# Two tiles of stores in flight, the router judged inside attention's loop, later rests of W2, other row sums on TensorE: one change to a macaron layer (mixture of experts, linear attention, mixture of experts)

## The reference, cut to what matters

```python
def ffn(x):                                # x: [1024, 256]
    shared = silu_and_mul(x @ shared_gate_up_w.T) @ shared_down_w.T    # 704 wide
    shared = shared * sigmoid(x @ sgate_w.T)
    w = softmax(x @ gate_w.T)              # 16 experts
    topk_w, topk_ids = top_k(w, 4)
    for e in range(16):                    # w13_e: [352, 256], w2_e: [256, 176]
        coef = sum(where(topk_ids == e, topk_w, 0.0), axis=-1)
        acc = acc + (silu_and_mul(x @ w13_e.T) @ w2_e.T) * coef
    return shared + acc

x = x + 0.5 * ffn(layernorm(x))
x = x + attention(layernorm(x))            # q, k, v of 2 heads x 128, chunked scan,
x = x + 0.5 * ffn(layernorm(x))            # rmsnorm, Wo
```

## Time and profile before

| what | value |
|---|---|
| median of 3 runs | 455.74 us (454.93 to 457.75) |
| the profiled execution | 455.48 us |
| its span, first to last instruction | 453.7 us |
| TensorE busy | 410.8 us, 91% |
| VectorE busy | 300.4 us, 66% |
| ScalarE busy | 202.1 us, 45% |
| GpSimd busy | 188.9 us, 42% |
| mean granted TensorE clock | 0.951 |
| bytes moved by DMA | 68.17 MB, mean 150 GB/s |

### The profile page before, as it was taken

One profiled execution on the slowest core, in us unless ns is written; L12 is line 12 of the kernel. 1 busy time (PEld: TensorE's weight loads), 2 busy tenths in 40 slices (PEclk: granted clock), 3 DMA queues, 4 the chain that ended last, 5 costly groups with the idle time before them and its releaser, 6 DMA issues.

```text
span 453.7 us, 8744 instructions
## 1 busy us (share of the span) xinstructions
PE 410.8 (91%) x2236; PEld 330.4 (73%) x2239; DVE 300.4 (66%) x943; ACT 202.1 (45%) x564; POOL 188.9 (42%) x199
## 2 busy tenths in 40 slices
PE   5998993699999999978969989689989999999995
PEld 3555552599999999553649975355569999999954
DVE  5666986377777776367596545645767777777637
ACT  2224562266666666124755632001126666666610
POOL 0174846044445445330055300767514544544542
PEclk9988997699999999989998976989999999999999
DMA  7999941344444441660000029422244444444167
GB/s 248 332 281 386 344 136 66 105 136 139 136 148 137 138 144 66 245 252 2 0 0 1 1 73 372 170 104 103 79 119 137 136 138 148 132 145 141 68 242 258
DMA packets 41023, 68.17 MB, mean 150 GB/s; under 512 B 5072, under 2 KB 32208, under 8 KB 40976
## 3 DMA queue, kind: packets, MB, share of 16 engines
q1 hardware_dynamic: 33392, 45.84, 32.4%
q0 software_dynamic: 7584, 21.77, 13.6%
HBM read 42.42 MB, written 25.17 MB: 149 GB/s over the span
## 4 chain that ended last, share of the span: by engine, by line
PE 70%; issue 7%; POOL 6%; DVE 6%; DMA 6%; ACT 3%; SPq 1%; DVEq 0%; POOLq 0%
PE ps L486 7%; PE ps L487 7%; PE ps L490 7%; POOL slots L907 6%; PE ps L426 6%; PE ps L449 5%; PE ps L471 5%; PE ps L431 4%; PE ps L519 3%; PE ps L514 2%; PE ps L518 2%; PE ps L516 2%; PE ps L515 2%; PE ps L497 2%; PE ps L498 2%
## 5 line engine op out<-in xcount | busy, mean ns | idle before, releaser
L914 POOL DMA_INDIRECT rows<-ar,idx x94 | 89.8, 955 | 118.0 <-ACT ar L762 117.4
L907 POOL DMA_INDIRECT slots<-XR,pos x64 | 70.1, 1096 | 76.5 <-DVE pos L1084 41.6
L486 PE MATMUL ps<-WH,xt 128*128 x188 | 69.2, 369 | 0.0
L487 PE MATMUL ps<-WL,xt 128*128 x188 | 61.1, 327 | 0.0
L1127 DVE SCALAR_TENSOR_TENSOR ar<-ps,XR,ar 128x112 f32<-128x112 f32 x94 | 31.4, 334 | 37.9 <-ACT ar L756 37.7
L1143 DVE TENSOR_TENSOR xl<-ps,xt 128x256 fp32r<-128x256 f32 x94 | 39.9, 424 | 24.2 <-ACT xt L751 10.6
L449 PE MATMUL ps<-WS,ar 128*128 128x256 f32 (+1 forms) x192 | 48.4, 399 | 8.1 <-DVE ar L996 7.4
L449 PEld LDWEIGHTS ps<-WS,ar 128*128 128x128 f32 (+1 forms) x192 | 37.3, 197 | 24.7 <-issue 12.9
L756 ACT ACTIVATE ar<-ps 128x176 f32<-128x176 f32 x94 | 29.9, 318 | 51.5 <-PE ps L490 51.5
L426 PE MATMUL ps<-XT,WS 128*128 128x512 f32 x96 | 50.8, 656 | 1.0 <-ACT sgt L739 1.0
L745 ACT ACTIVATE ar<-ps 128x512 f32<-128x512 f32 (+1 forms) x24 | 14.3, 596 | 80.3 <-PE ps L426 80.3
(11 more groups left out here) (171 smaller groups left out, 855.3 us busy)
## 6 DMA issues: line engine op xcount, KB each, us to landing
XR<-slots SPq DMA_DIRECT2D x94, 144.0 KB, 2.1
WR<-w SPq DMA_DIRECT2D x8, 1408.0 KB, 17.1
WR<-rows SPq DMA_DIRECT2D x16, 512.0 KB, 7.3
slots<-zeros SPq DMA_DIRECT2D x1, 2304.0 KB, 12.6
MR<-w2r SPq DMA_DIRECT2D x2, 1024.0 KB, 19.3
MR<-w2m SPq DMA_DIRECT2D x1, 1792.0 KB, 14.3
rows<-ar,idx POOLq DMA_INDIRECT x94, 2.4
X<-x SPq DMA_DIRECT2D x4, 256.0 KB, 4.6
```

The lines of the kernel that those rows point to most:

```text
L486: pe.matmul(to, token, WH[:, bass.ds(e, 1), k, :].rearrange("p a n -> p (a n)"), start=k == 0, stop=False)
L487: pe.matmul(to, token, WL[:, bass.ds(e, 1), k, :].rearrange("p a n -> p (a n)"), start=False, stop=False)
L907: pool.indirect_dma_start(out=slots_dram[:, :], out_offset=bass.IndirectOffsetOnAxis(ap=pos[:, t, r:r + 1], axis=0), in_=XR[:, t, :], in_o ...
L914: pool.indirect_dma_start(out=rows_dram[:, :], out_offset=bass.IndirectOffsetOnAxis(ap=idx[:, i:i + 1], axis=0), in_=ys[i % NY], in_offset ...
```

## The change

**Stores two tiles behind.** `BREAKS` goes. The stores of even and odd tiles count on two semaphores, and before tile t GpSimd waits for the stores of tile t - 2 (and earlier ones of that parity). There are six such waits in a pass where there were two.

**Opening of a pass.** In the first pass `places(0, 0)` comes ahead of the scaling of tiles 4 to 7 on VectorE. TensorE does `ranks(f, 0)` between the two products of unit 0 (`between`). The choice for the second half comes behind unit 0 on VectorE, its places and the table of tiles behind unit 1, `tables` behind unit 3.

**Router in the loop.** `judge(1, 0)` moves to turn 9 of attention's loop on VectorE, `router(1, 0)` to turn 10 on ScalarE.

**Late rests of W2.** `W2_LAST` has three pieces. Experts 0 to 3 stay at unit 7; 4 to 9 and 10 to 15 (`main(8)`, `main(9)`) go on ScalarE ahead of the slots, and on VectorE into the first turn of the slots. VectorE's `shared_sums(f, 1, FRONT)` moves from ahead of the slots to behind the first `left`. TensorE's 8 warming products now also run in the first pass.

**Tail.** TensorE sums the rows of tiles 2 and 3 in the first pass, into banks 0 and 1, between the last `unit_in` and the last two `unit_out`; in the second pass still those of tiles 4 and 5 at the end. Attention's weights come in three loads between the rows, TensorE waits for keys, queries and the rest one by one, and no longer for X of tile 5 before the queries. `gather` is the part of `combine` that makes the sum in SBUF, placed by itself. ScalarE's `norm` asks for the rates of tiles 2 and 3 ahead of the copies of tiles 0 and 1.

```diff
-W2_LAST = {7: (0, 4), 8: (4, NE)}
+W2_LAST = {7: (0, 4), 8: (4, 10), 9: (10, NE)}
-BREAKS = (3, 6)
-BY_PE = (4, 5)
+BY_PE = ((2, 3), (4, 5))
...
-                sp.wait_ge(s_disp, 16 * NT * TOPK * (f + 1))
+                for b in range(2):
+                    sp.wait_ge(s_disp[b], 16 * TOPK * HT * (f + 1))
...
                     if f == 0 and t == 3:
-                        sp.dma_start(WA[:, :, :], wkqv).then_inc(s_wa, 16)
+                        sp.dma_start(WA[:, :, 0:D], wkqv[:, :, 0:D]).then_inc(s_wk, 16)
+                    if f == 0 and t == 5:
+                        sp.dma_start(WA[:, :, D:2 * D], wkqv[:, :, D:2 * D]).then_inc(s_wq, 16)
+                    if f == 0 and t == 7:
+                        sp.dma_start(WA[:, :, 2 * D:], wkqv[:, :, 2 * D:]).then_inc(s_wa, 16)
                         sp.dma_start(WO[:, :, :], woT).then_inc(s_wa, 16)
...
             def rows_summed(f):
-                pe.wait_ge(s_uh, UNITS * (f + 1))
-                for n, t in enumerate(BY_PE):
+                for n, t in enumerate(BY_PE[f]):
...
-                unit_in(f, 0)
-                ranks(f, 0)
+                unit_in(f, 0, lambda: ranks(f, 0))
...
+                unit_in(f, 2)
                 ranks(f, 1)
-                unit_in(f, 2)
                 unit_out(f, 1)
+                unit_in(f, 3)
+                unit_out(f, 2)
                 over_partitions(f)
...
-                if f == 1:
-                    keep_warm(8, 6)
+                keep_warm(8, 6)
...
                 for u in range(FRONT + 1, UNITS):
                     unit_in(f, u)
+                    if f == 0 and u == UNITS - 1:
+                        rows_summed(f)
                     unit_out(f, u - 1)
                 unit_out(f, UNITS - 1)
-                rows_summed(f)
+                if f == 1:
+                    rows_summed(f)
...
             def norm(c):
                 rates(c, 0, 2)
-                for q in range(1, 4):
-                    copied(c, 2 * q - 2)
-                    copied(c, 2 * q - 1)
-                    rates(c, 2 * q, 2)
+                rates(c, 2, 2)
+                for t in range(4):
+                    copied(c, t)
+                rates(c, 4, 2)
...
                 for i in range(3, NT + 5):
                     step(i)
-                router(1, 0)
+                    if i == NT + 2:
+                        router(1, 0)
...
                     for t in range(HT * h, HT * (h + 1)):
-                        if t in BREAKS:
-                            pool.wait_ge(s_disp, 16 * TOPK * (NT * f + t))
+                        wait(pool, s_disp[t % 2], 16 * TOPK * (HT * f + t // 2))
...
                 left(0)
+                shared_sums(f, 1, FRONT)
...
+                    if f == 0 and i == 0:
+                        main(8)
                     if i < TL:
                         hidden(i, e[i])
+                    if f == 0 and i == 0:
+                        main(9)
...
             def ffn(f):
+                unit(f, 0)
                 choose(f, 1)
-                unit(f, 0)
+                unit(f, 1)
                 places(f, 1)
                 tiles_of(f)
-                unit(f, 1)
-                tables(f)
...
-                shared_sums(f, 1, FRONT)
                 slots(f)
...
-                judge(1, 0)
+                    if i == NT + 1:
+                        judge(1, 0)
...
+            places(0, 0)
             for t in range(HT, NT):
                 scale(0, t)
-            places(0, 0)
```

More of the change, by code:

```diff
@@ L428, in unit_in @@
                 mm.then_inc(s_ug, 1)
+                if between:
+                    between()
                 if not last:
@@ L999, in unit, with main @@
                 ins.then_inc(s_uh, 1)
+            def main(u):
+                dve.wait_ge(s_mh, list(W2_LAST).index(u) + 1)
+                for e in range(*W2_LAST[u], 2):
+                    two = slice(e, e + 2)
+                    ins = dve.tensor_tensor(ML[:, two, :], MR[0:FM, two, :], MH[:, two, :].bitcast(F32), ALU.subtract)
+                ins.then_inc(s_ml, 1)
             def part(f, u):
@@ L1007, in part @@
                     ins.then_inc(s_rl, 1)
[L1008 to L1013 removed]
+                if f == 0 and u == 7:
+                    main(u)
                 for e in range(*PARTED.get(u, (0, 0))):
@@ L1223, in ffn @@
                     judge(f, 1)
+                unit(f, 0)
                 choose(f, 1)
-                unit(f, 0)
+                unit(f, 1)
                 places(f, 1)
                 tiles_of(f)
-                unit(f, 1)
-                tables(f)
-                for u in range(2, NJ + 1):
+                unit(f, 2)
+                part(f, 2)
+                for u in range(3, NJ + 1):
                     unit(f, u)
+                    if u == 3:
+                        tables(f)
                     part(f, u)
```

80 lines of the change are left out of this document (48 added, 32 removed).

## The result

| | us | ratio to before |
|---|---|---|
| forecast | 443.2 (438.2 to 449.2) | 0.973 |
| before, beside the changed kernel | 455.34 | 1 |
| changed, first measurement | 483.53 median, 477.63 to 490.43 in 4 runs | 1.051 [1.043, 1.060] |

Medians are of all runs; ratios, and the intervals behind them, compare only the runs that the chip didn't slow down. The same kernel was measured four more times, on chips 9, 2, 10 and 5: 0.981, 0.964, 0.983 and 1.077. So there are two things to explain: what the change is worth where the forecast's picture holds, and the 35 to 45 us that the first and the last of the five measurements add.

The account below looks back on a forecast made before the run. TensorE bounds the slots; the first dispatch, second dispatch and first tail decide the rest. 455.48 - 8.1 (first dispatch) + 2.8 (first slots) - 2.8 (first tail) - 4.2 (second dispatch) = 443.2 us, range 438.2 to 449.2.

Parts of the forecast that it names:

- TensorE's own front: Before the first slot: TensorE's earlier work, with warming products, would end at 73.7, ahead of the slot's start at 75.4.
- E: Rival: stores land in 9.0 us in both dispatches, GpSimd waits before every tile; 457.2 us, chance 3%.
- First dispatch, 8.1 us forecast: First pass's stores: earlier start 1.3 plus drains 9.0 less new waits 2.2; first slot at about 75.4.
- Start 1.3: First dispatch: places come about 1.3 us earlier, no longer behind four scalings and unit 0's second product.
- Drains 9.0: First dispatch: the two drain waits go, 4.32 + 4.69 = 9.0 us.
- New waits 2.2: First dispatch: six waits for stores two tiles back cost 2.2 us in all, bounds 0 and 8.1.
- rival C: VectorE holds GpSimd more than before: two more long stores beside weight splitting cost 3.9 us; 447.1 us, chance 9%.
- First slots, 2.8 given back: First slots: 5.35 us of moved VectorE work, about 2.5 fitting its room, loses 2.8 us.
- First tail, 2.8: First pass's tail: VectorE's 3.9 us wait for ScalarE's rates goes, less 1.1 for a collision; gains 2.8 us.
- the one collision of 1.1: First tail: VectorE held once beside GpSimd's adds of tiles 6, 7, costing 1.1 us, bounds 0 and 2.2.
- Second dispatch, 4.2: Second pass's stores: start 2.0 sooner, drains 2.9 gone, about 0.7 given back in the slots; net 4.2 us.
- The rest at nothing: Second tail, extra DMA issues and tables behind unit 3 were put at no cost or gain.

Follow-up runs that it names:

- e12: Kernel before, unchanged, run again on chip 2 for its profile: 449.96 us, 1.002 of the kernel before.
- e11: Kernel before with only the waits two tiles behind in place of the drains, chip 2: 439.39 us, 0.976 of the kernel before.
- e14: Changed kernel, unchanged, on chip 5: 487.37 us, 1.077 of the kernel before.
- e5: Changed kernel, unchanged, on chip 9: 440.43 us, 0.981 of the kernel before.
- e6: Changed kernel with late rests of W2 and shared sums put back ahead of the slots, chip 9: 436.57 us, 0.970 of the kernel before.
- e10: Same kernel as e6, measured again on chip 2: 434.87 us, 0.967 of the kernel before.
- e16: As e15, with both tails put back too, chip 5: 482.41 us, 1.069 of the kernel before.
- e15: Same kernel as e6, measured again on chip 5: 483.91 us, 1.069 of the kernel before.
- e8: Changed kernel with the opening's order, early rests of W2 and shared sums all put back, chip 9: 443.94 us, 0.986 of the kernel before.
- e17: As e15, with the second pass's router also put back behind attention's loop, chip 5: 484.53 us, 1.063 of the kernel before.
- e2: Kernel before with only the waits two tiles behind in place of the two drains, chip 12: 440.44 us, 0.981 of the kernel before.
- e18: Same kernel as e2, measured again on chip 3: 440.95 us, 0.983 of the kernel before.
- e4: Changed kernel with 12 GpSimd memsets added before tiles 3 and 6, chip 12: 456.77 us, 1.014 of the kernel before.

## Why the prediction was wrong, point by point

Three traces from chip 2 give the terms their sizes: the kernel before (e12, 454.80 us), the waits alone (e11, 444.39) and the changed kernel (e9, 441.29). The fourth row is e14. Times in us from the timelines: the first and last store's issue, the start of the first slot's turning and the end of the last one's, and the same for the second pass.

| | stores, pass 1 | first slot | last slot's turning | stores, pass 2 | first slot | span |
|---|---|---|---|---|---|---|
| e12 before | 21.6 to 76.8 | 82.2 | 174.4 | 278.4 to 326.4 | 331.6 | 452.9 |
| e11 waits alone | 21.1 to 64.7 | 71.9 | 168.9 | 274.2 to 315.7 | 323.8 | 442.6 |
| e9 changed | 19.8 to 62.1 | 71.7 | 167.3 | 271.2 to 312.7 | 317.9 | 439.5 |
| e14 changed, chip 5 | 20.4 to 60.4 | 93.6 | 190.4 | 290.8 to 330.0 | 363.2 | 484.4 |

The span shrinks by 13.4 us from e12 to e9; the forecast was 12.3. That the two lie so close is in part luck. The stages that the change was to shorten gained 16.6 us, as the paragraphs below count, and the second slots 0.4. Two stretches that were put at nothing took back 3.5: the second tail 0.7, and attention 2.8. Attention, from the last scaling of the first tail to the last one before the second dispatch, takes 56.3 us in e12 and 59.1 in e9. The change isn't shown to be the cause: it takes 58.8 in e11, where attention is that of before, and 55.4 in e5, where it is the changed one.

**The step that failed** is the one on TensorE's own front, which "must be over" before the first slot: "its last product ended at 72.0", and with the warming products at 73.7. It was taken over from the trace of before, as if the engines' work among themselves could not be touched by stores that no longer stop. In the first measurement and on chip 5 TensorE's signals reach ScalarE and VectorE up to 28.5 us late, TensorE waits for these two in turn, and the front stands still for 20 to 25 us a pass: the first slot starts at 94.72 and not at 75.4. What holds the signals stays open. None of the rivals held this: E, the one for slower, put the price into GpSimd's waits for landings, and these were 1.0 us in all. Its 3%, and the 2% for slower, were too small for a mechanism nobody had measured: three engines run for 40 us beside a stream of 32 stores that the trace of before shows only in pieces of 12 and 8.

**First dispatch, 8.1 us forecast.** Start 1.3: 21.6 to 19.8, 1.8. Drains 9.0: right, both waits are gone. New waits 2.2: one of 0.91, so 0.6. Also gone is most of GpSimd's lost time beside splitting, which rival C feared would grow. Before, on chip 2, rows with their durations and idle times:

```profile
41.22 0.96 POOL L907 DMA_INDIRECT slots<-XR,pos  x1 [4.63 <-DMA slots<-XR,pos]
...
61.96 0.96 POOL L907 DMA_INDIRECT slots<-XR,pos  x1 [4.75 <-DMA slots<-XR,pos]
...
64.71 2.91 POOL L907 DMA_INDIRECT slots<-XR,pos  x1 [0.30 <-issue]
...
71.38 0.96 POOL L907 DMA_INDIRECT slots<-XR,pos  x1 [2.49 <-issue]
72.65 2.64 POOL L907 DMA_INDIRECT slots<-XR,pos  x1 [0.30 <-issue]
```

and in e9:

```profile
30.69 0.96 POOL L921 DMA_INDIRECT slots<-XR,pos  x1 [0.91 <-DMA slots<-XR,pos]
...
54.28 2.04 POOL L921 DMA_INDIRECT slots<-XR,pos  x1 [0.30 <-issue]
```

The earlier dispatch is over before most of the splitting begins, so the last store comes 14.8 us sooner, not 8.1. But the first slot gains only 10.5: now TensorE's front is the limit, and its warming products run right up to the first slot.

**First slots, 2.8 given back.** Right in kind, a little small: first to last slot takes 95.6 us against 92.2, 3.4 more. e9's stretches (columns as above), and TensorE's and VectorE's timelines there:

```profile
75.50:79.50 4.00, 1.88 (x8) 1.59 (x9) 4.00 (x10) 0.85 (x3) 0.00 (x0) 0.82 0.06 7
79.50:83.50 4.00, 4.00 (x24) 3.53 (x22) 3.61 (x13) 1.59 (x5) 0.51 (x1) 0.75 0.23 67
```

```profile
75.78 0.59 PE L494 MATMUL ps<-WH,xl 128*128 x2 [0.71 <-DVE xl L1160]
78.21 0.46 PE L501 MATMUL ps<-cst,ar 128*112 128x128 f32 x1 [1.85 <-DVE ar L1148]
...
80.35 0.95 PE L494 MATMUL ps<-WH,xl 128*128 x2
```

```profile
73.73 1.66 DVE L1041 SCALAR_TENSOR_TENSOR X<-ps,gate,X 128x256 f32<-128x256 f32 x4 [0.49 <-issue]
...
75.64 1.89 DVE L1019 TENSOR_TENSOR ML<-MR,MH 112x512 fp32r<-112x512 f32 x3
...
78.07 1.89 DVE L1019 TENSOR_TENSOR ML<-MR,MH 112x512 fp32r<-112x512 f32 x3
```

VectorE is busy 4.00 of 4.00 and TensorE waits 0.71 + 1.85 = 2.6 us for it; behind the pause the granted clock reads 0.82 and 0.75, and a pair of L494 takes 0.95, for 0.48 at full clock: this one ran at the lower of the two levels, 1.2 GHz. I put the remaining 0.8 down to that clock, which the forecast left to the range. e11, without the late rests, shows that the term isn't theirs alone: 97.0 us, because its slots start at 71.9, before VectorE has finished its splits, and TensorE waits 3.29 us for them. With the rests put back under the new opening (e6, e10) the slots take 92.3 and 92.1, but they start later too, at 73.3 and 77.3. To the last slot's end the changed kernel gains 7.1 us here, forecast 8.1 - 2.8 = 5.3.

**First tail, 2.8.** Too large. From the last slot to the last scaling: 37.4 us in e12, 36.2 in e11, 36.4 in e9: 1.0, and nothing against the waits alone. The wait for rates is gone, as forecast, but the one collision of 1.1 was two of a dearer kind. In the changed kernel of the first measurement:

```profile
214.90 2.76 POOL L967 TENSOR_TENSOR WR<-WR 128x512 f32<-128x512 f32 x2 [6.91 <-DMA WR<-rows]
```

```profile
212.50 0.72 DVE L1002 TENSOR_SCALAR XR<-X,mv,rstd 128x256 f32<-128x256 f32 x2
...
215.30 3.26 DVE L1002 TENSOR_SCALAR XR<-X,mv,rstd 128x256 f32<-128x256 f32 x2
```

Two scalings of 0.72 took 3.26 beside GpSimd's adds, 2.5 in place of 1.1. The rows of tiles 6, 7 land when they land, and VectorE, now early, meets the adds. The Trainium skill, "SBUF — State Buffer", section "Who interferes with whom", has VectorE and GpSimd exclude each other where a VectorE instruction reads two inputs in SBUF, and also where a TENSOR_SCALAR runs in a mode that takes both ports. These scalings read one tensor in SBUF and two scalars per partition; the row agrees that a TENSOR_SCALAR can be held, and doesn't show in which mode it ran. e16, with the old tail, takes as long from its last slot to its last scaling as e15 (36.1 and 36.2 us in single traces). Their times lie within 2 us of each other, but with intervals as wide as theirs (1.057 to 1.081) these don't tell 2.8 us from nothing.

**Second dispatch, 4.2.** Too small. The start, from the last scaling to the first store, takes 10.3 us in e12 and 8.5 in e9, so 1.8 for the forecast 2.0; with the opening put back (e8) it is 10.2 and with the router put back (e17) 10.3, against 8.2 in e15, as if it took both. But this stretch varies by 2 us between traces of one kernel (8.2, 10.4 and 8.2 in e2, e11 and e18), so these single traces don't show it. From its first store to its first slot: 53.3 us in e12, 46.6 in e9, 6.7 for the forecast 2.2. What was missing are pauses of GpSimd that aren't waits for landings. e12's second dispatch:

```profile
295.07 0.96 POOL L907 DMA_INDIRECT slots<-XR,pos  x1 [1.77 <-DMA slots<-XR,pos]
...
307.94 2.88 POOL L907 DMA_INDIRECT slots<-XR,pos  x1 [0.30 <-issue]
...
314.59 1.25 POOL L907 DMA_INDIRECT slots<-XR,pos  x1 [2.51 <-DMA slots<-XR,pos]
...
322.64 0.96 POOL L907 DMA_INDIRECT slots<-XR,pos  x1 [2.98 <-issue]
```

The two drains hold 1.47 + 2.21 = 3.7 us, and the 2.98 before a store that waits for nothing, 2.7 over the usual 0.30, is gone in e9: 6.4 of 6.7. Only the first 0.9 us of that pause lies beside a split of VectorE; what held the rest isn't shown. The 0.7 that were to be given back in the second slots don't show: 91.6 us in e9, 92.0 in e12. In e11, with the old opening, 49.5 us pass: TensorE's front, not the stores, is the limit there, and the new opening brings the other 2.9.

**The rest at nothing.** The second tail takes 30.0 us in e9 against 29.3 and 27.9 in e12 and e11. GpSimd's last adds there, which wait for the rows, start 10.7 us after its first ones in e9 and 8.3 in e11, but also 10.0 in e12 and 8.4 in the first trace of the kernel before. So I can't put the difference down to the change.

**The chances.** As ratios to 455.5 us the range is 0.962 to 0.986. Three measurements of five lie in it (0.981, 0.964, 0.983); the first one and the one on chip 5 lie far above, where 2% of the chances were.

## What to carry to other kernels

A pause that looks like pure waiting may be what keeps another engine's signals on time; these runs make one suspect it and don't show it. Before taking drains out of a long stream of indirect stores, measure on more than one chip, and measure the unchanged candidate beside every variant. When a wait is released by nothing that the core did, look for engines that resume in the same instant, and compare the time at which a semaphore is raised with the end of the instruction that raises it. And when GpSimd's stores and VectorE's two-input work overlap, count the overlap: with 8.8 us of drains gone the first dispatch on chip 2 became 13.0 us shorter.

## What the runs showed of the hardware that I had not expected

- TensorE's signals to ScalarE and VectorE can arrive 10 us and more late (28.5 at most), and in the order of its products, while GpSimd issues 32 indirect stores 1.27 us apart; those of the other engines were late by 1.8 us at most. In four of the five traces that show it, ScalarE and VectorE then resume within 0.14 us of each other, 4.2 to 5.9 us after the last store's issue began. By their times, all 20 executions of kernels without drains in the first measurement and on chip 5 had it; no trace from chips 12, 9, 2, 10 and 3 shows it.
- The stores themselves are not slowed: the first dispatch with late releases is the shortest (40.0 us in e14, 42.3 in e9); no store there is a long one, while VectorE stands still.
- An indirect store of 0.96 us takes 2.0 to 3.6 us beside VectorE's two-input splits (2.04 in e9, 3.58 in e6); a dispatch that is delayed meets more of them (four such stores in e4, none in the first measurement's trace).
- One kernel differs by up to 6.6 us between measurements on different chips: the kernel before took 448.8 on chip 12 and 455.3 in the first measurement. The times of different chips are never subtracted here.
- Attention varied between traces of the same changed kernel, without late releases to explain it: 55.4 us in e5, 59.1 in e9.
